# One attention-and-FFN block on one core: units' largest weights two heads later, tops ahead of blocks, first value and row weights at the loop's end

## What is computed

```
x = x + layernorm(attention(layernorm(x), Wq, bq, Wk, bk, Wv, bv, Wo, bo, gq, gk))
x = x + layernorm(ffn(layernorm(x), W_base, b_base, W_gate, W_thr, b_thr, A, B))

attention(x):
    q, k, v = x @ Wq + bq, x @ Wk + bk, x @ Wv + bv        # 512 -> 4096 = 32 heads of 128
    q, k = rms_norm(q, gq), rms_norm(k, gk)                # over all 4096 columns
    out = softmax(q k^T / sqrt(128)) v                     # by head
    return out @ Wo + bo
ffn(x): a 512x512 layer plus 8 gated experts of rank 16
```

## Time and profile before

| | us |
|---|---|
| median of three executions | 1101.89 |
| profiled execution | 1103.57 |
| span of its instructions | 1101.5 |
| PE busy in the span | 1062.8 (96%) |
| DVE busy | 794.2 (72%) |
| ACT busy | 727.3 (66%) |
| POOL busy | 678.6 (62%) |

### The profile page before, as it was taken

How to read it: one execution, slowest core, us unless ns; L and a number is a source line. 1 busy time by engine, 2 the same in 40 slices (tenths; PEclk the granted TensorE clock), 3 DMA queues, 4 the chain that set the end, 5 groups by cost and what they waited for, 6 DMA issues and landing times.

```text
span 1101.5 us, 19973 instructions
## 1 busy us (share of the span) xinstructions
PE 1062.8 (96%) x5724; PEld 577.2 (52%) x5724; DVE 794.2 (72%) x1801; ACT 727.3 (66%) x1427; POOL 678.6 (62%) x593
## 2 busy tenths in 40 slices
PE   6999999999999799999999999999999999999896
PEld 3444444444444465555555555555555555555385
DVE  7867666666644777777777777777777777777886
ACT  3567666666655677776777777777777677767432
POOL 2578767667665376766766666666667667664413
PEclk9999999999999899999999999999999999999998
DMA  6777755655664388687766766775775775776502
GB/s 232 167 264 244 241 219 198 228 217 199 234 147 131 108 210 211 185 175 171 190 171 168 194 172 162 193 177 157 191 183 155 191 182 159 184 167 150 162 1 76
DMA packets 311635, 197.39 MB, mean 179 GB/s; under 512 B 275248, under 2 KB 279216, under 8 KB 311472
## 3 DMA queue, kind: packets, MB, share of 16 engines
q1 hardware_dynamic: 311600, 196.97, 64.5%
HBM read 94.14 MB, written 35.68 MB: 118 GB/s over the span
## 4 chain that ended last, share of the span: by engine, by line
PE 63%; issue 14%; POOL 14%; DVE 4%; DMA 2%; ACT 2%; POOLq 1%; SPq 0%; DVEq 0%
PE ps L1095 21%; PE ps L1096 21%; PE ps L1097 21%; POOL acc L582 10%; POOL qk_out L573 3%; DMA vo_top_scratch<-top_o 1%; DVE stats L1429 1%; DMA wv_stage<-w_vo 1%; DVE y L1908 1%; POOL wb_lo L727 0%; DMA y<-x 0%; DVE y L1794 0%; DVE ps L1811 0%; ACT pair_q L926 0%; ACT ps L917 0%
## 5 line engine op out<-in xcount | busy, mean ns | idle before, releaser
L1811 DVE TENSOR_SCALAR_CACHE_REDUCE ps<-ps,score_down 128x512 f32<-128x512 f32 x256 | 177.6, 756 | 95.3 <-PE ps L1097 94.8
L1825 DVE SCALAR_TENSOR_TENSOR pair_q<-ps,row_inv,pair_q 128x512 f16<-128x512 f32 x256 | 174.6, 744 | 56.7 <-ACT pair_q L926 54.4
L1095 PE MATMUL ps<-xh,wa_hi 128*128 128x512 f16 x512 | 195.0, 381 | 6.1 <-DVE qk_out L1639 3.8
L917 ACT ACTIVATE ps<-ps,neg_max 128x512 f32<-128x512 f32 x256 | 168.2, 657 | 48.1 <-DVE ps L1811 48.1
L1097 PE MATMUL ps<-xh,wa_lo 128*128 128x512 f16 x512 | 195.1, 381 | 0.0
L1096 PE MATMUL ps<-xl,wa_hi 128*128 128x512 f16 x512 | 195.1, 381 | 0.0
L926 ACT ACTIVATE pair_q<-ps,row_inv 128x512 f16<-128x512 f32 x256 | 154.9, 688 | 20.2 <-DVE row_inv L1818 19.9
L675 POOL CAST oth<-o_t 128x512 f16<-128x512 f32 x62 | 37.8, 610 | 210.1 <-ACT o_t L902 210.1
L582 POOL TENSOR_TENSOR acc<-acc,squares 128x512 f32<-128x512 f32 x120 | 150.1, 1272 | 0.0
L1095 PE MATMUL ps<-wv_hi,xh 128*128 128x256 f16 x512 | 139.6, 273 | 0.0
L1097 PE MATMUL ps<-wv_hi,xl 128*128 128x256 f16 x512 | 139.6, 273 | 0.0
(11 more groups left out here) (184 smaller groups left out, 2221.8 us busy)
## 6 DMA issues: line engine op xcount, KB each, us to landing
q_k_scratch<-qk_out SPq DMA_DIRECT2D x64, 512.0 KB, 4.0
qk_in<-q_k_scratch SPq DMA_DIRECT2D x64, 512.0 KB, 3.4
wa_stage<-w_qk SPq DMA_DIRECT2D x32, 512.0 KB, 4.0
u_stage<-w_vo SPq DMA_DIRECT2D x32, 512.0 KB, 5.0
wv_stage<-w_vo SPq DMA_DIRECT2D x16, 512.0 KB, 4.2
wo_stage<-w_vo SPq DMA_DIRECT2D x16, 512.0 KB, 4.1
qk_tops<-qk_top_scratch SPq DMA_DIRECT2D x28, 128.0 KB, 4.6
y<-x SPq DMA_DIRECT2D x8, 256.0 KB, 5.5
```

The lines of the kernel that those rows point to most:

```text
L917: act.activation(ps[:, SCORE + i, :], ps[:, SCORE + i, :], ACT.Exp, bias=neg_max[:, sl, i:i + 1], scale=-1.0, accum_out=row_sum[:, sl, i:i ...
L1095: pe.matmul(outp, lhs[0], rhs[0], start=first, stop=False)
L1811: dve.tensor_scalar(ps[:, SCORE + i, :], ps[:, SCORE + i, :], score_down[:, sl, i:i + 1], None, ALU.mult, ALU.min, accum_out=neg_max[:, sl ...
L1825: dve.scalar_tensor_tensor(out=pair_q[:, 1, i, :], in0=ps[:, SCORE + i, :], scalar=row_inv[:, sl, i:i + 1], in1=pair_q[:, 0, i, :], op0=AL ...
```

## The change

Three things are altered in the projection phase.

- `largest_of_unit` moves two heads later on DVE. Ahead of the loop only units 0 and 1 are reduced, in the loop head h reduces unit h in place of unit h + 2, and units 30 and 31 come behind the loop, ahead of `largest_out`. The loads of the units move by two heads likewise: SP loads unit h + 1 in head h instead of h + 3, and unit 31 after the last store of head 29.
- `load_tops` stands first in SP's part of a head, ahead of the loads of the head's weights and of the unit. Ahead of the loop the reduction, store and load of the tops of heads 4 and 5 come earlier.
- The first blocks of `wv_stage` and `wo_stage` are loaded at the end of SP's loop and one head behind it, not ahead of the loop; ACT gets a wait for each before the first use.

```diff
-            def phase_a(i, o, weights=True, tops=True, top=True, unit=True):
+            def phase_a(i, o, weights=True, tops=True, top=True):
                 h, par = 4 * i + o, o % 2
+                if tops:
+                    load_tops(h + 3, 1 - par)
                 if weights:
                     sp.wait_ge(wa_lo_ready, 2 * h + 4)
                     load_wa(h + 5, (o + 1) % 4)
-                if unit:
-                    load_unit(h + 3, 1 - par, h + 3)
-                if tops:
-                    load_tops(h + 3, 1 - par)
+                load_unit(h + 1, 1 - par, h + 1)
                 if top:
                     store_tops(h + 4, par)
...
             store_qk(0, 0, 0, 1)
+            store_tops(4, 0)
             sp.wait_ge(wa_lo_ready, 6)
             load_wa(6, 2)
-            load_unit(2, 0, 2)
-            store_tops(4, 0)
+            load_tops(4, 0)
+            store_tops(5, 1)
             store_qk(1, 1, 0, 2)
             store_qk(0, 0, 1, 3)
-            load_unit(3, 1, 3)
-            load_tops(4, 0)
-            store_tops(5, 1)
+            load_unit(2, 0, 2)
             store_qk(1, 1, 1, 4)
-            load_unit(4, 0, 4)
-            sp.dma_start(wv_stage[:, :, :].rearrange("p c n -> p (c n)"), w_vo[0]).then_inc(wv_loaded, 16)
-            sp.dma_start(wo_stage[:, :, :].rearrange("p h n -> p (h n)"), w_vo[PAIRS]).then_inc(wo_loaded, 16)
             with sp.Fori(1, PAIRS // 2 - 1) as i:
                 for o in range(-2, 2):
                     phase_a(i, o)
+            sp.dma_start(wv_stage[:, :, :].rearrange("p c n -> p (c n)"), w_vo[0]).then_inc(wv_loaded, 16)
             phase_a(PAIRS // 2 - 1, -2)
+            sp.dma_start(wo_stage[:, :, :].rearrange("p h n -> p (h n)"), w_vo[PAIRS]).then_inc(wo_loaded, 16)
...
-            phase_a(PAIRS // 2 - 1, 1, weights=False, top=False, tops=False, unit=False)
+            phase_a(PAIRS // 2 - 1, 1, weights=False, top=False, tops=False)
+            load_unit(HEADS - 1, 1, HEADS - 1)
...
                     if b == 0:
-                        largest_of_unit(h + 2, par, 16 * (2 * i + o // 2 + 2))
+                        largest_of_unit(h, par, 16 * (2 * i + o // 2 + 1))
...
-            largest_out()
             dve.wait_ge(stored[0][0], 16 * (PAIRS - 1))
             dve.wait_ge(k_cols_ready, 3 * HEADS)
+            largest_of_unit(HEADS - 2, 0, 16 * PAIRS)
             store_k(0, 0, 2, 8 * PAIRS - 6)
+            largest_of_unit(HEADS - 1, 1, 16 * PAIRS)
+            largest_out()
```

More of the change, by code:

```diff
@@ L858, in _ @@
             act.wait_ge(v_up_ready, 1)
+            act.wait_ge(wv_loaded, 16)
             split_wv(0, 0, 0)
@@ L962, in first_steps @@
                 act.wait_ge(o_up_ready, 1)
+                act.wait_ge(wo_loaded, 16)
                 split_wo(0, 0, 0)
@@ L1653, in _ @@
             store_k(0, 0, 0, 2)
-            largest_of_unit(0, 0, 16)
+            largest_qk(4, 0, 0, 32)
             low_wa(2, 2)
             first_factors(3)
-            largest_qk(4, 0, 0, 32)
             store_k(1, 0, 1, 4)
-            largest_of_unit(1, 1, 16)
+            largest_qk(5, 1, 1, 32)
             store_k(0, 1, 0, 6)
             low_wa(3, 3)
-            largest_qk(5, 1, 1, 32)
-            largest_of_unit(2, 0, 32)
+            largest_of_unit(0, 0, 16)
             store_k(1, 1, 1, 8)
-            largest_of_unit(3, 1, 32)
+            largest_of_unit(1, 1, 16)
             def largest_value():
```

## The result

The changed kernel took 1108.98 us, the median of five executions (1108.4 to 1113.09), beside 1103.08 us for the kernel before on the same chip (five, 1100.92 to 1105.58): 5.9 us slower by the two medians. The record's ratio of the two kernels, which is not the quotient of the medians, is 1.0079 (95% interval 1.0058 to 1.01), or 8.7 us. So it is clearly slower, by 6 to 9 us. The profiled executions stand 4.8 us apart (1108.40 and 1103.57), their spans 5.1 us (1106.6 and 1101.5).

What follows compares the result with a forecast made beforehand. PE bounds projection and attention, so only its idle stretches at 50–110 and 325–385 us count. 1103.57 - 2.57 + 2.0 = 1103.0 us profiled; against the median, 1101.89 - 0.57 = 1101.3 us, range 1098.7 to 1104.3.

Steps and rivals of the forecast that it cites:

- Front, -2.57: From 50 to 110 us: head 4's tops come 3.6 us sooner, so both PE stalls go, winning 2.57 us.
- In the loop the tops' load comes ahead of the weights and the unit ... I cost this at nothing: PE's full busy time hides it.: Projection loop: the new load order costs nothing, since PE is fully busy and DVE has idle time.
- a late landing would cost what it is late, some tenths: DVE's wait for tops_v until 331.23 us: costed at nothing, transfers ahead unchanged; a late landing costs some tenths.
- Seam, +2.0: From 325 to 385 us: unit 31 delays top_o's issue 4.6 us; its later landing costs PE 2.0, ends 0 and 4.6.
- The fixed cost of a store: top_o's store: the skill's about 2 us would land it at about 351 us, seam free; measured 9.4 us speaks against.
- Clock, nothing: PE's granted clock in the seam: a longer idle time adds nothing, with 1 us kept either way.
- The whole delay: Rival for the seam: top_o takes 9.4 us from issue, landing 4.6 us late; 1104.0 us, chance 0.15.

Runs made afterwards that it cites:

- f2: Changed kernel, tops read behind the loads again, units 30 and 31 loaded into free weight slots and reduced in the loop: 1099.08 us, 0.9978 of the kernel before.
- f1: The changed kernel run once more, unedited, on another chip: 1110.24 us, 1.0082 of the kernel before.
- h1: Kernel before with only the tops' load moved to the front of SP's part of a head, on another chip: 1110.29 us, ratio 1.0086.
- e2: Kernel before with only the tops' load moved to the front of SP's part of a head: 1128.96 us, ratio 1.0198.
- h3: Kernel before with SP's wait for the column store's landing at the front of a head, tops' read left in place: 1102.19 us, ratio 0.9998.
- e1: Changed kernel with the tops' load again behind the loads of weights and unit: 1107.12 us, 1.0002 of the kernel before.
- e3: Changed kernel with units 30 and 31 neither loaded nor reduced: 1123.17 us, 1.0155 of the kernel before.
- f4: Kernel before with each head's column store held until the key store may go: 1100.89 us, ratio 0.9991.
- g4: f2 with top_v stored and tops_v read one head earlier, column store held, value weights loaded ahead of the wait for top_o: 1097.44 us, 0.9938 of before.
- e4: Kernel before with largest_out on DVE moved behind the second of the last four keys: 1110.7 us, ratio 1.0037.
- g1: Changed kernel with each head's column store held until the first key store may go: 1105.57 us, 1.0051 of the kernel before.
- g3: Kernel before with the second pair's value weights loaded ahead of SP's wait for top_o's landing: 1099.7 us, ratio 0.9983.

## Why the prediction was wrong, step by step

The profiled executions give the sum by stage. At PE's last stall of the projection the changed kernel was 0.19 us late (forecast: 2.57 early), the seam cost 3.36 us (2.0), the clock behind it gave back 1.70 us (0) and the FFN cost 3.2 us (0): 5.1 us against a forecast of -0.57.

**Front, -2.57.** Right in mechanism and size. The stalls went (no stall from 50 to 110 us), and f2, whose last stall comes 2.6 us sooner than in before, is 2.7 us faster.

**"In the loop the tops' load comes ahead of the weights and the unit ... I cost this at nothing: PE's full busy time hides it."** This is the step that failed. I looked at PE and DVE, which had time, and not at SP and its queue, though the rows for it were at hand: 5.6 us of landing for the column and a head of 10.3 us. The moved line carries a wait for that landing, and all of SP's transfers of a head stand behind it. That closes a circle: tops' read, weights, unit, column, its landing, next tops' read. SP waits at this line in every head, so that the spacing of the tops' reads is the circle's length: 10.42 us in the changed kernel (120.03 to 318.04 us, 19 heads), 10.32 in f1, 10.53 in h1, 11.14 in e2. PE needs 10.3 us for a head (48 matmuls, 0.215 us each). At 10.3 it costs nothing in the loop. A little above it SP falls further behind PE in each head, nothing stalls, and the delay comes out at `tops_v`; at 11.1 the circle is the pace of the loop. h3 shows that it is the read's place in the queue and not the wait that makes the circle so long; e1 that the place of the tops is worth about 8 us to the changed kernel (1.0079 and 1.0082 against 1.0002, from different chips).

**"a late landing would cost what it is late, some tenths" (`tops_v`).** The same step at its end. The landing of `top_v` grew by 2.8 us, and the last stall by 3.3 us. The prediction had named this as what would make it wrong, but costed it by the transfers around it, and not by the state of SP that the loop would leave. Its premise, that the transfers ahead of that load are the same as before, did not hold: the order in the loop is another, and the two 512 KB loads of `wv_stage` and `wo_stage` now stand ahead of `top_v`. e1 keeps those two and lands `top_v` in 8.8 us, so it was the order.

**Seam, +2.0.** The mechanism was right, the term too small. Unit 31 was reduced at 346.69 us (forecast 346.5), `top_o` issued at 348.14 (347.95); it landed in 7.5 us, not 6.35, the load behind it took 6.68 in place of 6.02 us, and PE restarted 3.55 us late. Taken from PE's last stall it is 26.54 us against 23.18, 3.4 us. On A the term was larger: 28.05 us in e1 against 23.1 in e3; there it ate the whole front gain. That the landing counts from something else than its issue was right: it was 7.5 us here and 9.1 in e1, where it was issued 3.8 us earlier.

**The fixed cost of a store.** The prediction held the measured 9.4 us against a cost of 2 us. In the runs a column store of the loop landed in 3.0 us at the median where it stood clear of the loads (f4 and g4, single ones in 2.6 us), and in 4.9 to 9.1 us elsewhere; the stores of `top_v` and `top_o` took 7.2 to 14.6 us. The Trainium skill, page "DMA: Bandwidth & Descriptors", section "Anatomy of one DMA", gives its fixed cost of about 2 us for transfers through GpSimd's path. The stores here go through SP, so that no run tests the figure; as a price for them it would be too low in every place. An estimate by that page's figure is 347.95 + 2 = 350 us, not the 351 us that the prediction names. The Trainium skill's section "Queues, rings and completion order" on the same page says that the signal of completion is a write that lands only after every earlier write of the same DMA engine. The changed kernel's 8.5 us right behind two loads agree with a wait for what is ahead, but the runs don't test the rule by itself.

**Clock, nothing.** More than the 1 us kept either way: 1.7 us came back behind the seam, where the granted clock was 1.00 from 382 to 388 us, and some 2.3 us were lost to it in the FFN.

**The rivals.** The whole delay, at 1104.0 us, came nearest, and of its 4.65 us the seam took 3.4. But no rival had the loop in it, so none reached the 1109 us measured: the range's upper end was the seam's worst case with the front gain kept.

**What is left open.** What moved the fall of the clock and the landing of `x` in the FFN is not shown. PE waits 4.10 us for `z` at 1050 us where it waited 1.53, and its transposes then take 3.67 in place of 1.97 us. Among the eighteen profiles this pair takes two values: a wait of 3.2 to 4.2 us with transposes of 3.4 to 3.7 in eight, 0.4 to 1.8 us with 1.97 in ten. Six of the eight have the tops in front, but e4 and h3 have the long wait without that, and e3 and g1 have the tops in front and the short one. It was not tried by itself. Also open is why the circle is 11.1 us on one chip and 10.5 on another for the same kernel, and where the slower executions of f1 lose their time.

## What to carry to other kernels

A wait that is moved to the front of an in-order queue must be costed as a circle: from the transfer behind the wait, through all that it holds back, to the event that it waits for in the next round. If the circle is near the length of the round, the busiest engine's full busy time hides nothing, and the cost of the same line may be 9 us on one chip and 22 on another (e2 and h1). It need not appear in the loop: look at the first small transfer behind it that somebody waits for. Here a store whose landing is awaited did best well behind the large loads, and what doesn't need the landing should be issued ahead of the wait (g3). Before work is moved behind a loop, look for a buffer that is free inside it (f2).

## What the runs showed of the hardware

- The landing of a 128 x 2 column store to HBM went with what it followed: medians of 3.0 us when issued 5.3 us behind a 512 KB load (f4), 5.3 at 1.7 us (before), 8.5 at 0.5 us (after). With the broadcast ahead of the loads it is longer: 6.3 us at 2.7 us (g1). The 512-byte column store of `top_v` took 8.8 (e1) to 14.6 us (e3).
- The 128 KB broadcast read of one 1 KB row took about 1 us of the engines behind two large loads, and some 2 us in front of them (f1), with a DMA share of 0.94 to 1.14 at 34 to 82 GB/s.
- The DMA share is no measure of work: the loop moved 212 and 214 GB/s at shares of 0.63 and 0.89.
- One line in another place cost the same kernel 1.0198 on one chip and 1.0086 on another, with intervals of 0.002 to 0.003 each way, while the kernel before differed by only 0.4% between these chips.
